# A state-space scan: four silus and four gates in one stretch of ScalarE, and the first series one slot later

## What is computed

```python
x = jnp.einsum('bld,ed->bel', hidden_states, in_proj_w)
xc = conv(x, conv_w)                       # 4 taps along the positions
x = silu(xc + conv_b[None, :, None])
x_dbl = jnp.einsum('bdl,ed->bel', x, x_proj_w)
dt_low, Bm, Cm = jnp.split(x_dbl, [dt_rank, dt_rank + d_state], axis=1)
dt = softplus(einsum('brl,dr->bdl', dt_low, dt_proj_w) + dt_proj_b)
def step(state, inp):
    d, b, c, u = inp
    state = state * jnp.exp(d[..., None] * A) + (d * u)[..., None] * b[:, None, :]
    return (state, jnp.einsum('bdn,bn->bd', state, c))
y = (y + D[None, :, None] * x) * silu(z)   # z: the layer norm of the input
```

## Time and profile before

| | |
|---|---|
| median of three runs | 1582.73 us (1582.67 to 1585.43) |
| the profiled execution | 1584.61 us |
| its span, first to last instruction | 1582.6 us |
| busy in the span: PE, DVE, ACT, POOL | 1452.8, 1143.0, 975.5, 528.9 us |
| the scan's first slots to its last | 48 to 460 us |

### The profile page before, as it was taken

How to read it: one execution, slowest core, us unless ns; L and a number is a source line. 1 busy time by engine, 2 the same in 40 slices (tenths; PEclk the granted TensorE clock), 3 DMA queues, 4 the chain that set the end, 5 groups by cost and what they waited for, 6 DMA issues and landing times. The chain is left out here.

```text
span 1582.6 us, 21472 instructions
## 1 busy us (share of the span) xinstructions
PE 1452.8 (92%) x6244; PEld 634.7 (40%) x6245; DVE 1143.0 (72%) x1672; ACT 975.5 (62%) x1544; POOL 528.9 (33%) x334
## 2 busy tenths in 40 slices
PE   6788978989979999999999798898999999999999
PEld 2344434434434444444444343332333333344444
DVE  7999999999995422222223769889899999637885
ACT  3999999999964011111112532587878878877764
POOL 0679689688971620000003655505000000000000
PEclk7799999989989999999999899999999999999999
DMA  5212313114114494457524635453232232230464
GB/s 188 71 51 88 93 47 115 52 43 121 60 34 175 173 224 153 146 200 268 182 92 140 220 100 159 152 184 95 72 94 74 75 92 72 60 107 14 86 138 123
DMA packets 142519, 183.41 MB, mean 116 GB/s; under 512 B 55491, under 2 KB 89667, under 8 KB 141427
## 3 DMA queue, kind: packets, MB, share of 16 engines
q1 hardware_dynamic: 120918, 134.58, 29.0%
q0 software_dynamic: 6624, 23.14, 4.8%
q10 hardware_dynamic: 14912, 24.89, 4.6%
HBM read 109.29 MB, written 54.92 MB: 104 GB/s over the span
## 5 line engine op out<-in xcount | busy, mean ns | idle before, releaser
L274 POOL TENSOR_TENSOR m_hs<-m_hs,m_C 128x1024 f32<-128x1024 f32 x128 | 302.1, 2378 | 75.7 <-DVE m_hs L496 75.1
L1827 DVE TENSOR_REDUCE a_mx<-a_s 128x2 f32<-128x1024 f32 x256 | 303.4, 1218 | 27.3 <-PE a_s L1943 23.8
L496 DVE TENSOR_TENSOR_SCAN m_hs<-m_dA,m_d 128x512 f32<-128x512 f32 x256 | 293.5, 1199 | 8.1 <-PE m_d L651 7.2
L651 PE MATMUL m_d<-ident_sb,m_dBuT 128*128 128x128 f32 x1024 | 160.2, 289 | 27.9 <-DVE m_hs L496 21.4
L651 PEld LDWEIGHTS m_d<-ident_sb,m_dBuT 128*128 128x128 f32 x1024 | 116.3, 145 | 154.0 <-DVE m_hs L496 81.6
L380 ACT ACTIVATE m_dA<-m_dt,m_negA 128x512 f32<-128x512 f32 x256 | 167.7, 710 | 8.0 <-DMA m_dt<-m_dt 6.5
L1281 PE MATMUL e_gu<-e_w,e_xgT 128*128 x376 | 169.1, 592 | 0.0
L358 ACT ACTIVATE m_dBuT<-m_dtuT,m_BT 128x512 f32<-128x512 f32 x241 | 157.6, 710 | 0.1
L1943 PE MATMUL a_s<-ring_sb 96*128 96x512 bf16 x512 | 150.1, 383 | 7.0 <-DVE a_mx L1827 2.7
L946 ACT ACTIVATE e_sg<-e_gu 128x256 f32<-128x256 f32 x47 | 18.0, 383 | 223.0 <-PE e_gu L1281 223.0
L666 PE MATMUL m_y<-m_hs,m_fold 128*64 128x512 f32 x512 | 142.1, 635 | 0.4 <-POOL m_hs L274 0.2
(11 more groups left out here) (334 smaller groups left out, 2433.7 us busy)
## 6 DMA issues: line engine op xcount, KB each, us to landing
e_w<-in_ex_gu SPq DMA_DIRECT2D x16, 1024.0 KB, 6.6
ring_sb<-qk_dram SPq DMA_DIRECT2D x64, 192.0 KB, 3.1
xg_dram<-zeros_sb SPq DMA_DIRECT2D x47, 256.0 KB, 3.0
e_xg<-xg_dram ACTq DMA_DIRECT2D x47, 256.0 KB, 2.6
yg_dram<-attn_sb ACTq DMA_DIRECT2D x47, 256.0 KB, 2.1
m_C<-c_dram SPq DMA_DIRECT2D x64, 128.0 KB, 2.9
m_dt<-m_dt SPq DMA_DIRECT2D x64, 128.0 KB, 2.4
e_w<-in_ex_dn SPq DMA_DIRECT2D x16, 512.0 KB, 8.5
```

The lines of the kernel that those rows point to most:

```text
L274: pool.tensor_tensor(hs[:, J % RH], hs[:, J % RH], C2[:, N % RC].unsqueeze(1).broadcast_to([P, 2, L]), ALU.mult).then_inc(s_hc, 1)
L496: dve.tensor_tensor_scan(hs[:, J % RH, h], dA[:, j % RA], pd[j % RD][:], 0.0, ALU.mult, ALU.add)\
L651: last = pe.transpose(pd[j % RD][:, t * P:(t + 1) * P], dBuT[:, N % 2, t, g], ident[:])
L1827: dve.tensor_reduce(mx[:, r % 2, h * TB + 2 * c:h * TB + 2 * c + 2], psc[c][:], AX.X, ALU.max)\
```

## The change

Before, ScalarE computed the first two silus and the four gates in slot 3 and the other two silus in slot 5, each with a load of the silu's table ahead and of the Exp's behind. Now all eight stand in slot 5. In slot 3 only batch 0's Sqrt is left. The gates of batch 3, which has no silus, move to slot 5 with the others. The first `series_first` of a batch moves from slot 12 to 13, where the first `series_last` stands already; the other three series keep their slots.

```diff
@@ -410,12 +410,10 @@
                     if b == 0:
                         act.wait_ge(s_ln, LN_VAR)
                         act.activation(rstd[:], rstd[:], ACT.Sqrt).then_inc(s_sd, 1)
+                if s == 5:
                     if p < B:
-                        silu(p, (0, 1))
+                        silu(p, range(E4))
                     gates(b)
-                    act.preload_act_table_set("natural_log_exp_and_others")
-                if s == 5 and p < B:
-                    silu(p, (2, 3))
                     act.preload_act_table_set("natural_log_exp_and_others")
                 if p < B:
                     if s == 8:
@@ -549,7 +547,7 @@
                     ln_columns()
                 if p < B and 1 <= s <= E4:
                     convolve(p, s - 1)
-                if p < B and s in (12, 15, 18, 21):
+                if p < B and s in (13, 15, 18, 21):
                     series_first(p, (s - 12) // 3)
                 if p < B and s in (13, 16, 19, 22):
                     series_last(p, (s - 13) // 3)
```

## The result

| | before | after |
|---|---|---|
| median (8 runs each) | 1584.72 us | 1588.90 us (1586.80 to 1590.23) |
| ratio, 95% interval | | 1.0026 (1.0016 to 1.0036) |
| ratio in a second measurement, on another chip (12 runs) | | 1.0024 (1.0011 to 1.0036) |
| span of the profiled execution | 1582.6 us | 1585.0 us |
| end of the scan: start of the last product with a gate | 464.08 us | 468.85 us |

Five more runs of before moved its median from 1582.73 to 1584.72. ScalarE has 6 us less to do, as counted, and the kernel is 4.1 us slower by the first ratio and 3.8 by the second (before had a median of 1597 us on that chip). The profiled execution of the changed kernel was the fastest of its eight, 1586.80 us, so the two spans differ by less than the two medians.

What follows compares the result with a forecast made beforehand. VectorE was taken to bound the scan; later second series in batches 0 to 2 and batch 3's delay, 0.27 + 0.66 + 1.84 + 0.46 = 3.2 us, added to the median 1582.73 gave 1585.9 us, range 1581.5 to 1589.

Steps and rivals of the forecast that it cites:

- What bounds: In the scan, VectorE sets the pace, with waits of 14 us in 412; a change counts by its effect on these.
- The loads taken away: On ScalarE in the scan, five table loads fewer, 6.4 us less work by the trace.
- drain: Further 1380 ns per table switch given by the skill, not shown by the trace; with it five loads would be worth 13 us.
- The wait for slot 4: ScalarE waits some 3 us for slot 4's scans before the silus; slot 6's inputs start 8.78 us after these scans in batch 1.
- The moved series pays for the late ScalarE in batch 1 and no more: VectorE reaches slot 14's scans at 213.28, as before, though ScalarE is 1.39 us later.
- The second series: In slot 15, VectorE waits 0.6 to 0.8 us for the logarithm; loss 0.66 us in batch 1, 1.84 in batch 2.
- Batch 3: Only gates move; slot 6's inputs come 0.46 us later, and TensorE's wait of 0.91 us becomes 1.4.
- Batch 0: The fourth silu waits for its convolution, ending 79.71; slot 6's inputs 1.04 us later, VectorE's second series 0.27 us later.
- rival 3: TensorE's clock falls behind two series in a row, up to 1 us more in three batches: 1588.9 us; chance 0.16.
- rival 1: ScalarE's saving reaches VectorE and the first-logarithm waits, 5.4 us, go entirely: 1577.3 us; chance 0.07.
- rival 2: No change: VectorE's second series has some tenths more room, so batches 0 and 1 lose nothing: 1583.5 us; chance 0.17.

Runs made afterwards that it cites:

- e7: The changed kernel measured again without edits, on a second chip; ratio 1.0024 (1.0011 to 1.0036) against before, end of scan 470.4 us.
- e1: The kernel before with only the first series moved from slot 12 to 13, silus and gates as before; ratio 0.9990 (0.9977 to 1.0003).
- e2: The changed kernel with the first series back in slot 12, so only silus and gates in one stretch; ratio 1.0039 (1.0020 to 1.0059) against before.
- e8: The kernel before run again without edits, for a second trace on the second chip; end of scan 467.9 us, profiled execution 1603.10 us.
- e10: Repeat of e4 on a third chip; ratio 0.9975 (0.9965 to 0.9986) against before, median 1581.45 us.
- e11: Repeat of e1 on a third chip; ratio 0.9984 (0.9975 to 0.9994) against before, median 1583.11 us.
- e9: The changed kernel with ten decay buffers instead of eight (lead still three slots), gates ahead of silus, product with D ahead of turns; ratio 0.9954 against before.
- e5: The changed kernel with TensorE's product with D of slots 1 to 4 ahead of its slot's turns; one execution, end of scan 469.0 us.
- e4: The changed kernel with slot 5's stretch ahead of slot 8's decays and gates ahead of silus; ratio 0.9990 (0.9975 to 1.0005) against before.

## Why the prediction was right, and where it wasn't

- **What bounds.** VectorE's waits were the right place to look: of the 4.8 us by which the scan of the first trace ended later, 3.9 are idle time of VectorE.
- **The loads taken away** were five, and ScalarE's busy time fell by 5.9 us (6.4 counted). No drain showed behind a load; the next instruction follows 1.30 us after its start.
- **The wait for slot 4.** 2.77 us in batches 1 and 2, forecast "some 3"; in batch 0 2.08 and, in e7, 2.75. The sum from the end of the scans to the inputs of slot 6 was 8.78; measured 8.77 (192.43 - 183.66), and 8.77 in batch 2.
- **The moved series pays for the late ScalarE in batch 1 and no more.** Between the scans of slot 4 and those of slot 14: before 33.72, after 33.71. e1 and e2 show the two sides apart, -0.8 and +1.4 at the places named.
- **The second series.** Waits of 0.57 us; the batch's loss 0.64 (forecast 0.66) and 1.79 in batch 2 (1.84). Batch 3: TensorE's wait 1.39 (1.4), the loss 0.52 (0.46); with e7 and e8 it is 0.21, since the end of this batch varies by a microsecond by itself.

The row of batch 3 on TensorE, against the last of the earlier trace rows:

```profile
403.46 1.09 PE L649 MATMUL m_d<-ident_sb,m_dBuT 128*128 128x128 f32 x8 [1.39 <-ACT m_dBuT L358]
```

- **Batch 0 was the step that failed.** "The fourth silu would start at 79.50, but its convolution ends at 79.71" left out a third condition in the code, the product with D, and took one execution's clock as given. 0.27 forecast, 1.85 in the first trace; with it the sum is 4.8, which is the later end of the scan in this pair of traces. In the pair e7 and e8 the scan ended 2.5 us later. So the 4.8 fits one pair; how far batch 0 was missed in the median isn't known.
- **From the scan to the end.** The profiled span grew by 2.4 us only, because the stages behind the scan took 1118.5 us in the profile of before and 1116.1 in that of after. In other profiles on chips of that speed they took 1117.8 (e10), 1118.5 (e11) and 1118.8 (e9). On the second chip the same kernel took 1129.2 us there in e7, and 1133.1 in e5, which changes nothing behind the scan. So a single span has 2 to 4 us of play that no edit explains; the difference of the medians, 4.2 us, lies between the two pairs' 4.8 and 2.5.
- **The time.** 1585.9 was forecast and 1588.90 measured. Of these 3.0 us, 2.0 are the median of before, which rose with five more runs; the difference was forecast as 3.2 us and is 4.2. The measured time is that of rival 3, 1588.9, and that is chance: the clock behind the two series cost nothing. It also lies only 0.1 us inside the upper side of the range. The prediction itself gave "slower" 0.46 and "no change" 0.47, so the way it moved was worked out rightly, but not called with confidence.
- **The rivals.** The gain (rival 1) needed the inputs of slot 6 earlier behind the end of the scans than before, 7.4 us in batch 1 and 6.2 in batch 2; they came at 8.8. In e9 they come at 5.1, earlier in both, and in e4 at 6.3, earlier in batch 1 alone. The rule of the Trainium skill, "ScalarE: Activation LUTs", section "Table sets: the hidden batching unit", to batch calls by set, is thus borne out in the loads saved, and not in the time where the batch stands behind this wait. Cover (rival 2) did not occur. Of the clock (rival 3) the fall behind the two series occurred, and the loss did not; clock losses of about a microsecond came elsewhere, in the kernel before as well (e8).

## What to carry to other kernels

Putting work together saves the switches between its parts, but it also ties all of it to the latest thing that any part, or anything queued ahead of it, waits for. Before moving a long stretch on an engine that runs ahead of its consumer, find the wait that will stand in front of it, and put in the time of that wait what needs neither side. And price an edit by the position of the next work behind it, not by the engine's busy time: here 6 us less of work made 4 us more, and the same work in another order made 4 us less, of which by e11 the moved series alone brings 2.5. And take an effect of a microsecond from more than one trace of each kernel.

## What I had not expected of the hardware

TensorE's granted clock did not fall in the same way in each execution. Around 74 us TensorE stands idle for 2.8 us and then does the projection of four matmuls. In both traces of before and both of after it did so at or near half clock for most of the time (3.2 to 3.8 us for the four, VectorE's wait behind them 1.04, 1.50, 1.63 and 1.44 us). In e10 the same idle of 2.80 us went before, and the clock stayed at full (2.4 GHz): 1.98 us for the four, and no wait. e1 shows the same. From 74 to 78 us, the changed kernel and then e10 (window, span, busy time of TensorE with count, granted clock, DMA share, GB/s):

```profile
74.00:76.00 2.00, 2.00 (x3) 0.50 0.00 1
76.00:78.00 2.00, 2.00 (x7) 0.50 0.00 0
```

```profile
74.00:76.00 2.00, 2.00 (x11) 1.00 0.01 4
76.00:78.00 2.00, 2.00 (x10) 1.00 0.52 173
```

A term that hangs on this clock has a spread of up to 1.6 us for one such place, and one trace does not give it.
